# Token columns by 32 by 32 block fetches and a VectorE transpose, gate weights kept on chip, and expert sums moved and split in a two-layer attention and mixture-of-experts kernel

## The reference

```python
x = x + attn_a(layernorm(x))   # causal, 16 heads of width 8
x = x + ffn(layernorm(x))      # mixture of experts
x = x + attn_b(layernorm(x))   # 16 heads, scores from q.k with per-head norms
x = x + ffn(layernorm(x))      # same weights again

def ffn(x):                    # per token; 8 experts, hidden width 512
    top_vals, top_idx = top_k(x @ Wr, 2)
    combine = softmax(top_vals) scattered to the 8 experts
    h = silu(x @ Wg[e]) * (x @ Wu[e])
    return sum_e combine[e] * (h @ Wd[e]) * 12 ** -0.5
```

## Time and profile before

| what | value |
|---|---|
| time, median of 3 runs | 1116.42 us (1113.54 to 1125.42) |
| the profiled execution | 1122.49 us, span on the core 1120.4 us |
| PE busy | 1004.0 us, 90% |
| DVE, ACT, POOL busy | 749.3, 675.4, 543.2 us |
| mean granted TensorE clock | 0.935 of full |

### The profile page before, as it was taken

How to read it: one execution, slowest core, us unless ns; L and a number is a source line. 1 busy time by engine, 2 the same in 40 slices (tenths; PEclk the granted TensorE clock), 3 DMA queues, 4 the chain that set the end, 5 groups by cost and what they waited for, 6 DMA issues and landing times.

```text
span 1120.4 us, 28587 instructions
## 1 busy us (share of the span) xinstructions
PE 1004.0 (90%) x9290; PEld 710.5 (63%) x9290; DVE 749.3 (67%) x2249; ACT 675.4 (60%) x1399; POOL 543.2 (48%) x764
## 2 busy tenths in 40 slices
PE   2999999999989999999798889999888899999990
PEld 1354555554568999999534444445544789999990
DVE  4697889877777333356778889998888753334542
ACT  2376777755644545555377779999778445455550
POOL 3143447634632710357776656588337155005465
PEclk9998999987989999999768889999889899999995
DMA  5444566534145977887743333343221578778973
GB/s 152 114 107 110 146 160 167 133 106 95 43 128 181 286 233 238 259 266 233 170 104 84 88 92 88 91 114 88 74 52 55 164 231 253 228 236 266 272 226 113
DMA packets 201721, 175.02 MB, mean 156 GB/s; under 512 B 19812, under 2 KB 160616, under 8 KB 201576
## 3 DMA queue, kind: packets, MB, share of 16 engines
q1 hardware_dynamic: 193384, 156.41, 50.6%
q0 software_dynamic: 8192, 16.79, 5.1%
HBM read 122.99 MB, written 50.14 MB: 155 GB/s over the span
## 4 chain that ended last, share of the span: by engine, by line
PE 61%; DVE 14%; SPq 8%; issue 6%; DMA 6%; POOL 3%; ACT 1%; POOLq 0%; DVEq 0%; ACTq 0%
PE psS L358 10%; PE psO L324 8%; PE psS L1399 7%; PE psT L1406 7%; DVE mx L664 5%; PE psS L389 4%; PE psN L1422 3%; PE psO L1422 3%; PE psM L279 3%; PE psN L331 3%; PE psT L366 2%; PE psM L429 2%; SPq L1476 2%; SPq L1471 2%; DMA xin<-xg 1%
## 5 line engine op out<-in xcount | busy, mean ns | idle before, releaser
L664 DVE TENSOR_REDUCE mx<-psS 128x3 f32<-128x384 f32 (+1 forms) x512 | 309.9, 618 | 88.7 <-PE psS L389 50.4
L358 PE MATMUL psS<-kst,qst 48*128 48x256 bf16 (+1 forms) x1024 | 195.8, 281 | 38.1 <-DVE mx L664 26.7
L561 ACT ACTIVATE pT<-psT,scb 128x512 f32<-128x512 f32 x256 | 192.5, 772 | 48.1 <-PE psT L366 46.0
L366 PE MATMUL psT<-qst,kst 50*128 50x256 bf16 (+1 forms) x1024 | 191.9, 274 | 4.1 <-DMA qst<-scr_m 1.8
L1463 DVE TENSOR_TENSOR hT<-sg,psT 128x512 f32<-128x512 f32 x142 | 97.5, 687 | 142.1 <-PE psT L1406 118.6
L1282 POOL DMA_INDIRECT xg<-xn,slot x128 | 123.2, 963 | 118.8 <-DVE ysb L1458 71.0
L1399 PE MATMUL psS<-xTt,wgc 128*128 128x128 f32 x1136 | 153.3, 278 | 3.7 <-issue 3.5
L556 ACT ACTIVATE pT<-psT 128x384 f32<-128x384 f32 x256 | 123.5, 489 | 54.8 <-PE psT L366 46.7
L1406 PE MATMUL psT<-xTt,wuc 128*128 128x128 f32 x1136 | 151.6, 277 | 1.1 <-DMA wuc<-in_L_ffn_Wu 1.1
L358 PEld LDWEIGHTS psS<-kst,qst 48*128 48x128 bf16 x1024 | 63.5, 96 | 138.1 <-DVE mx L664 71.6
L1296 POOL DMA_INDIRECT pT<-eo,slot x64 | 60.6, 947 | 175.3 <-DVE ysb L1458 105.5
(11 more groups left out here) (230 smaller groups left out, 1601.0 us busy)
## 6 DMA issues: line engine op xcount, KB each, us to landing
wgc<-in_L_ffn_Wg SPq DMA_DIRECT2D x142, 256.0 KB
wuc<-in_L_ffn_Wu SPq DMA_DIRECT2D x142, 256.0 KB
scr_part<-part SPq DMA_DIRECT2D x128, 128.0 KB, 2.1
qst<-scr_part SPq DMA_DIRECT2D x64, 192.0 KB, 3.7
kst<-scr_part SPq DMA_DIRECT2D x64, 192.0 KB, 4.6
xin<-xg SPq DMA_DIRECT2D x142, 64.0 KB
eo<-ysb SPq DMA_DIRECT2D x142, 64.0 KB
scr_part<-part SPq DMA_DIRECT2D x32, 192.0 KB, 1.9
```

The lines of the kernel that those rows point to most:

```text
L358: return nc.tensor.matmul(ps[:, c0:c0 + n], q_[r64, t, q0], k_[r64, t, 0:n], start=(half == 0), stop=True, skip_group_check=True)
L366: return nc.tensor.matmul(ps[:, c0:c0 + T - q0], k_[m64, t, half * P:half * P + P], q_[m64, t, q0:T], start=(half == 0 or not L.causal), s ...
L561: nc.scalar.activation(pT[:, g % 8, 0:cols], psT[g % 2][:, 0:cols], ACT.Exp, scale=scb[r][:, 0, i:i + 1], bias=scb[r][:, 1, i:i + 1]).then ...
L664: nc.vector.tensor_reduce(mx3[:, u, 0:n, pos:pos + 1].rearrange("p a b -> p (a b)"), psS[h % 2][:, 0:kcols(L)].rearrange("p (a k) -> p a k ...
```

## The change

**Tokens.** `sp_load` no longer fetches a tile of 128 rows of 512 bytes. It fetches two tiles at once (the first fetch one) in four DMAs, one for each 32 columns, each with pieces of 32 floats, so that block row f of the transposed tile lies in partitions 32f to 32f + 31 with its 32 by 32 blocks not yet transposed. One DVE instruction (`dve_columns`, 128 by 256) transposes the blocks into `xTt`. PE's transpose into psM and ACT's copy of it go, and with them the waits that kept psM apart from attention B's preparation.

**Gate weights.** The gate weights of all experts are loaded to SBUF once (`wg`, 8 DMAs of 256 KB in attention A), and ACT copies the tile's expert to `wgc` (`act_gate`); `sp_gate` becomes `sp_up` and fetches `wuc` only.

**Three parts.** Group 1's results come in three parts: blocks 0 to 8 after 57 tiles, 9 to 12 after 65, 13 to 15 after all 71. The counts have one more column set, the tables three ends, and route stage 8 is split into stages 8 to 11 at k = 6 to 9.

**Moves.** Group 0's gathers are issued two per tile and no longer 1.5; its sums begin up to four tiles earlier, and so do the moments of blocks 4 to 15. Attention B's four pieces of eight additions become eight of four at (3, 3), (3, 5), (4, 3), (4, 5), (6, 3), (6, 7), (7, 3), (7, 5). POOL's five gathers per step there all stand behind `pool_split`; before, one stood ahead of the chain and one ahead of the split. A few routing pieces of attention A move by one to two heads. The last store is split into one of one block and one of three.

```diff
+PARTS = (9, 13)
+OWN_A, OWN_B = (2 * (SIZE[0] + p) + E - 1 for p in PARTS)
+LAST_STORES = ((NBLK - 4, NBLK - 3), (NBLK - 3, NBLK))
...
+        wg = sb("wg", [P, E * HID])
-        xin = [sb(f"xin{i}", [P, D]) for i in range(FETCH)]
-        xTt = [sb(f"xTt{i}", [P, P]) for i in range(FETCH)]
+        xin = [sb(f"xin{i}", [P, 2 * D]) for i in range(2)]
+        xTt = [sb(f"xTt{i}", [P, 2 * P]) for i in range(2)]
...
             if k == ROUTE_LN:
                 dve.wait_ge((LA, LB)[l].s["x1"], NBLK)
+                dve_columns(dve, l, 0)
                 dve_ln_stats(dve, NBLK - 4, NBLK, s_ln[n])
+                dve_columns(dve, l, 1)
...
-            if k == ROUTE_SLOT + 1:
-                dve_route_part(dve, n, 8)
+            if ROUTE_SLOT + 1 <= k < ROUTE_SLOT + 5:
+                dve_route_part(dve, n, 8 + k - ROUTE_SLOT - 1)
...
                 if g == 1:
-                    link(nc.vector.tensor_tensor(out=further, in0=rank, in1=each(lim[2][:]), op=ALU.is_ge))
-                    link(nc.vector.tensor_tensor(out=further, in0=further, in1=each(step_b[:]), op=ALU.mult))
-                    link(nc.vector.tensor_tensor(out=b, in0=b, in1=further, op=ALU.add))
+                    for i in (1, 0):
+                        link(nc.vector.tensor_tensor(out=further, in0=rank, in1=each(lims[:, i + 1, :]), op=ALU.is_ge))
+                        link(nc.vector.tensor_tensor(out=further, in0=further, in1=each(steps[:, i, :]), op=ALU.mult))
+                        link(nc.vector.tensor_tensor(out=b, in0=b, in1=further, op=ALU.add))
...
             for pair in range(2 * SIZE[0]):
-                pool.wait_ge(f_sem["y"], n0 + OWN + 2 * pair // 3 + 1)
+                pool.wait_ge(f_sem["y"], n0 + OWN + pair // 2 + 1)
                 pool_gather(pool, 2 * l, pair)
-            for pair in range(2 * PART if l == 1 else 0):
-                pool.wait_ge(f_sem["y"], n0 + TILES - 4 * PART // 3 + 2 * pair // 3)
+            for pair in range(2 * PARTS[1] if l == 1 else 0):
+                pool.wait_ge(f_sem["y"], n0 + OWN_A)
                 pool_gather(pool, 3, pair)
...
-                nc.tensor.transpose(psM[:, 0:P], xin[i][:], ident[:]).then_inc(f["T_ps"], 1)
...
+        def act_gate(act, l, t):
+            n = l * TILES + t
...
+            chosen[n] = expert(act, l, t)
+            after(act, f_sem["g"], n - FETCH + 1)
+            nc.scalar.activation(wgc[n % FETCH][:], wg[:, bass.ds(chosen[n], HID)], ACT.Copy
+                                 ).then_inc(f_sem["wg"], 1)
...
-                nc.scalar.activation(xTt[(n0 + t) % FETCH][:], psM[:, 0:P], ACT.Copy).then_inc(f["xT"], 1)
...
+        def dve_columns(dve, l, m):
+            i, width = m % 2, P * len(tiles_of(m))
+            after(dve, f_ld[i], 64 * (PAIRS // 2 * l + m // 2 + 1))
+            after(dve, f_sem["u"], l * TILES + max(2 * m - 3, 0))
+            nc.vector.transpose(xTt[i][:, 0:width], xin[i][:, 0:width]).then_inc(f_sem["xT"], 1)
...
-            sp.dma_start(wgc[n % FETCH][:], A["L0_ffn_Wg"].rearrange("e c h -> (e c) h")[bass.ds(row0, P), :]
-                         ).then_inc(f_wg[n % FETCH], 16)
...
-            sp.dma_start(xin[n % FETCH][:], xg[t * P:(t + 1) * P, :]).then_inc(f_ld[n % FETCH], 16)
+            tiles = tiles_of(m)
+            rows = xg[tiles[0] * P:(tiles[-1] + 1) * P, :].rearrange("(t b) (f a) -> f b t a", b=SQ, a=SQ)
+            after(sp, f_sem["xT"], PAIRS * l + m - 1)
+            for f in range(D // SQ):
+                sp.dma_start(xin[m % 2][SQ * f:SQ * f + SQ, 0:P * len(tiles)].rearrange("b (t a) -> b t a", a=SQ),
+                             rows[f]).then_inc(f_ld[m % 2], 16)
...
+        SUMS_AT = (3, 4, 6, 7)
...
-                if l == 1 and j < 7:
-                    lo, hi = {0: (0, 1), 1: (1, 2), H: (2, 5)}[h]
+                if l == 1 and j < 7 and h == H:
...
-                if l == 1 and (j, h) in ((4, 9), (5, 9), (7, 2), (8, 4)):
-                    dve_combine_1(dve, 0, (4, 5, 7, 8).index(j))
+                if l == 1 and j in SUMS_AT and h in (3, 7 if j == 6 else 5):
+                    dve_combine_half(dve, 0, SUMS_AT.index(j), int(h > 3))
...
-            for q, first in ((1, 13), (2, 18), (3, 23)):
+            for q, first in ((1, 11), (2, 15), (3, 19)):
...
-                if 27 <= at < 32:
-                    for h in (2 * (at - 27), 2 * (at - 27) + 1):
+                if 23 <= at < 28:
+                    for h in (2 * (at - 23), 2 * (at - 23) + 1):
```

More of the change, by code:

```diff
@@ L36 @@
 FETCH = 3
+SQ = 32
+PAIRS = (TILES + 1) // 2
 EPS = 1e-5
@@ L155, in build @@
         wgt = [sb(f"wgt{g}", [P, 2, SIZE[g]]) for g in range(G)]
-        pci = sb("pci", [P, 2, E], I32)
-        upto = sb("upto", [P, 3, 2, E])
-        ends = sb("ends", [P, 4, E])
-        lim = [sb(f"lim{g}", [P, E]) for g in range(G + 1)]
-        above_b = sb("above_b", [P, E])
-        step_b = sb("step_b", [P, E])
+        pci = sb("pci", [P, 3, E], I32)
+        upto = sb("upto", [P, 3, 3, E])
+        ends = sb("ends", [P, 5, E])
+        lim = [sb(f"lim{g}", [P, E]) for g in range(G)]
+        lims = sb("lims", [P, 3, E])
+        offs = sb("offs", [P, 3, E])
+        steps = sb("steps", [P, 2, E])
         below = [sb(f"below{g}", [P, E]) for g in range(G)]
@@ L1014, in pe_route @@
         def pe_route(pe, l, k):
-            n, free = 2 * l + 1, l * TILES + k + 2
+            n = 2 * l + 1
             if k == ROUTE_T:
@@ L1169, in dve_route_part @@
                 link(nc.vector.tensor_tensor(out=w[:, 1, :], in0=w[:, 0, :], in1=e_, op=ALU.mult))
-            rank, total, part = counts[:, 0:size, :], counts[:, size, :], counts[:, size + 1, :]
+            rank, total, sums = counts[:, 0:size, :], counts[:, size, :], counts[:, size:size + 3, :]
+            own = 2 if g == 0 else 3
+            ints, free = pci[:, 0:own, :], lim[1][:].unsqueeze(1).to_broadcast([P, 3, E])
             a, b, further = ea_, eb_, lg[:, 0:size, :]
@@ L1341, in dve_combine_1, with dve_combine_half @@
         def dve_combine_1(dve, l, q):
-            dve.wait_ge(r_gat[QUADS[0] + q], 16 * 8 * (l + 1))
             for i in range(2):
-                for k in range(4 * q, 4 * q + 4):
-                    dve_add_expert(1, k, i)
-                dve.wait_ge(r_sem["x"], 2 * blocks(2 * l + 1) + 8 * q + 4 * (i + 1))
+                dve_combine_half(dve, l, q, i)
+        def dve_combine_half(dve, l, q, i):
+            if i == 0:
+                dve.wait_ge(r_gat[QUADS[0] + q], 16 * 8 * (l + 1))
+            else:
+                dve.wait_ge(r_sem["x"], 2 * blocks(2 * l + 1) + 8 * q + 4)
+            for k in range(4 * q, 4 * q + 4):
+                dve_add_expert(1, k, i)
         def tile_loop(step, eng, l, before=None, behind=None):
@@ L1359, in tile_loop, with tiles_of, pair_of @@
                     behind(eng, l, k)
+        chosen = {}
+        def tiles_of(m):
+            return (0,) if m == 0 else (2 * m - 1, 2 * m)
+        def pair_of(t):
+            return (t + 1) // 2, int(t > 0 and t % 2 == 0)
         def live(k, d):
@@ L1405, in pe_tile @@
                     cols = slice(hb * P, (hb + 1) * P)
-                    last = nc.tensor.matmul(psT[p][:, cols], wuc[n % FETCH][:, cols], xTt[n % FETCH][:],
+                    last = nc.tensor.matmul(psT[p][:, cols], wuc[n % FETCH][:, cols], tokens,
                                             start=True, stop=True, skip_group_check=True)
@@ L1518, in sp_ffn @@
                     sp.wait_ge(r_gat[q], 16 * 8 * l)
-            for t in range(3):
-                sp_load(sp, l, t)
+            for m in range(2):
+                sp_load(sp, l, m)
             for k in range(TILES + 3):
@@ L1543, in hook @@
             def hook(pool, j, h):
-                if l == 1 and j < 7:
-                    lo, hi = {0: (0, 1), 1: (1, 2), H: (2, 5)}[h]
+                if l == 1 and j < 7 and h == H:
                     first = AHEAD_PAIRS + 5 * (j - 2)
-                    for pair in range(first + lo, min(first + hi, 2 * SIZE[1])):
+                    for pair in range(first, min(first + 5, 2 * SIZE[1])):
                         pool_gather(pool, 1, pair)
@@ L1587, in sp_beside @@
                              A["L0_ffn_Wd"][e].rearrange("(k p) d -> p k d", p=P)).then_inc(s_wffn, 16)
+            if 4 <= j < 4 + E and point == 1:
+                e = j - 4
+                sp.dma_start(wg[:, e * HID:(e + 1) * HID], A["L0_ffn_Wg"][e]).then_inc(s_wg, 16)
             if j == 6:
@@ L1940, in _ @@
             pool_ffn(pool, 1)
-            for pair in range(2 * PART, 2 * SIZE[1]):
+            for pair in range(2 * PARTS[1], 2 * SIZE[1]):
                 pool_gather(pool, 3, pair)
@@ L1971, in _ @@
             dve_route_part(dve, 3, 2)
-            for q in range(QUADS[1]):
+            for q in range(QUADS[1] - 1):
                 dve_combine_1(dve, 1, q)
+            for lo, hi in ((SIZE[1] - 4, PARTS[1]), (PARTS[1], SIZE[1])):
+                if lo < PARTS[1]:
```

(8 more changed lines are left out.)

166 lines of the change are left out of this document (75 added, 91 removed).

## The result

| kernel | median | ratio to the kernel before, 95% interval |
|---|---|---|
| before | 1115.8 us (1111.6 to 1125.9) | 1 |
| changed | 1101.3 us (1092.0 to 1113.3) | 0.9858 (0.9833 to 0.9883) |

What follows compares the result with a forecast made beforehand. PE was taken to bound the ffn, with DVE and ACT close behind in attention B. Terms -15.6 + 4.7 - 2 - 2.5 - 12 - 11 + 1 = -37.4 took 1116.4 us to 1079; range 1064 to 1098.

Steps and rivals of the forecast that it cites:

- The grid: Both ffns: PE's transpose leaves each tile, 2.79 us becomes 2.68, 142 x 0.11 = 15.6 us gained.
- Any of these is hidden: Ffn tiles: ACT's new work of at most 2.5 us and DVE's transpose, about 0.35 us per two tiles, stay hidden.
- so its count stays: Ffn, SP's queue: four token instructions for two, no gate weight instructions for two, per pair; no cost.
- inside the ffn: Both ffns: fewer bytes in flight and stage 8 in four steps outweigh three more DVE operations, -2 us (+1 to -5).
- rival 2: Ffns: SP's issues or DVE's token waits delay hT or PE, losing the slot won; 1095 us, chance 10%.
- Small pieces: Ffn token DMAs: 512 pieces of 128 bytes a tile at 20 to 30 ns each, no loss.
- Rival 1: Ffns: DMA becomes the bound from 48 ns a piece; at 68 ns about 1170 us, chance 7%.
- Start of the ffns: First tiles of each ffn: DVE's wait for tokens delays layer norm and PE, +4.7 us for both layers (+1 to +7).
- End of ffn 0: End of ffn 0: moments of blocks 4 to 15 come four tiles earlier, shortening attention B's first wait, -2.5 us.
- Attention B: Attention B, steps 3 to 8: additions in halves of four shorten the steps, -12 us (-17 to -3).
- rival 3: Attention B: halves collide with POOL or DVE is the bound, little of the 12 arrives; 1088 us, chance 12%.
- The end: After the last ysb: last-group gathers start four tiles earlier without waits, last sums shorter, -11 us (-8 to -12).

Runs made afterwards that it cites:

- ACT's stores: The changed kernel with the stores of ysb issued from ACT's queue and no longer from SP's; 1081.7 us, 0.9724 of the kernel before.
- old tokens: The changed kernel with the kernel before's functions for tokens and gate weights; 1096.7 us, 0.9822; with ACT's stores as well 1090.8 us, 0.9773.

## Why the prediction was wrong

**The grid: right.** A tile is 2.68 us; with ACT's stores PE held it over fifty tiles in both ffns. The transposes' 15.6 us are there in the grid once the rest keeps up; the longer starts take 5.0 of them, so that new against old tokens gives 9.6 us in the profiles with ACT's stores.

**"Any of these is hidden", "so its count stays": wrong, and the largest miss.** I costed ACT and DVE in microseconds and SP in instructions, eight per pair of tiles before and after. In time and order it isn't the same: SP's own work went from 5.04 of 5.58 us to 5.13 of 5.36. The four token issues are one lump of 1.92 us, and SP's store, which waits for DVE, stands in the same queue ahead of the next weights. Tiles 10 to 60 lost 3.7 and 3.0 us more than before instead of gaining the 2 of "inside the ffn". Forecast for both ffns -15.4, profiles -6.8. That is rival 2, SP's issues holding up PE, to which I gave 10%; its price was the whole slot of 15.6, and about half was lost. The row of PE at 60.00 of 60.00 misled me: it is a full stretch in a stage that was already 3.6 and 4.3 us over its grid in its middle. With old tokens ACT's stores took such losses away, so the queue was behind them already.

**Small pieces: right in the outcome, too dear in the price.** From the window of 440 to 470 us (share 0.69, 10.5 tiles by PE's 253 instructions) I get at most (0.69 x 16 x 30 / 10.5 - 14.0 - 4.4) / 512 = 26 ns a piece (gathers not taken off), with the prediction's 109 and 34 ns for the other kinds. The single transfers recorded in the traces say it directly: in the ffns one of 128 bytes took 13 ns, one of 512 bytes 27 to 29 ns, against the 20 to 30 and 34 ns of the prediction. Rival 1 needed 48. The Trainium skill's rule of 512 bytes ("DMA: Bandwidth & Descriptors", Specifications; the prediction called it the quick reference) held in that a byte costs about twice as much in a piece of 128 bytes as in one of 512, but it didn't decide the time: the DMA share fell.

**DVE's transpose**: 0.44 us for 128 by 256, forecast 0.35. It was hidden once SP's queue was free; in the changed kernel DVE stood 67.0 us for its tokens, against "no wait for xin in the middle". **Start of the ffns**: forecast +4.7; tiles 0 to 10 lost 2.4 and 0.1 us more than before, and with SP free new against old tokens 3.7 and 1.3. The term was right, the trace of the changed kernel shows half of it. **End of ffn 0**: PE's wait is 0.78 us for 1.85, so 1.1 for 2.5.

**Attention B: mis-sized, -12 against -4.0.** The term stopped at step 8 and put what follows at nothing. Up to there it was nearly right: steps 4 to 8 gave 10.9 of 16.2, and with the 1.3 and 2.8 that were taken off for step 3 and for the half at (6, 7) it had -12. That half met the split as feared, 3.66 us or 0.92 each (I had 0.98), but I left out that the clock falls with such a wait. The 6.3 us that came back in the last stretch, which no part of the prediction looked at, are most of the miss. So rival 3, the collision, has the size (8 us) but not the mechanism. Why the clock is lower there stays open. The Trainium skill's port rule ("SBUF — State Buffer", practical consequences) agrees again: the same four additions take 1.12 us clean and 3.66 beside a GpSimd instruction with two SBUF operands.

**The end: right**, -10.7 for -11; no wait among the 32 gathers. **Attention A**: -2.5 for +1 in this pair of profiles, which proves nothing: over all profiles it took 323.7 to 331.7 us with the weight loads (mean 328.1) and 322.8 to 328.2 in the three without (mean 324.8), which is within the forecast's bounds of 0 and +4.

**The sum.** 1101 against 1079 is 22 us. The stages make 13 to 14: 8.6 in the ffns and 8.0 in attention B, less 3.5 in attention A. The other 8 to 9 come from carrying the profile's 6 us over the median to the changed kernel, whose profiled execution lay 2.6 us under its own; the executions of the changed kernel also had the lower mean clock (0.936 for 0.9425), for which the prediction had no term.

## What to carry to other kernels

Cost the DMA queue of an engine like an engine: issue time and register loads summed per round, against the round's length, and the order of what waits in it. A store that waits for a computation, ahead of loads that others wait for, belongs on another queue; here that one edit gave 15 us, about as much as the whole change. And a gain in a stage where PE's clock moves is not banked before the following stretch has been read at its granted clock.
